# Column sums of the last strip on the tensor engine, and degrees ahead of the split work, in a two-layer graph kernel

## The reference

```python
h  = relu(layernorm(x));  HW = h @ W                   # layer 0
A_norm = relu((adj + adj.T) * 0.5)
D = sum(A_norm, axis=1)
d_inv_sqrt = where(D > 0, D ** -0.5, 0)
L_norm = eye - d_inv_sqrt[:, None] * A_norm * d_inv_sqrt[None, :]
x  = x + relu(L_norm @ HW)
h  = relu(layernorm(x))                                # layer 1, three masks of adj
x  = x + diag(adj) @ (h @ W0) + triu(adj) @ (h @ W1) + tril(adj) @ (h @ W2) + bias
```

## Time and profile before

| | |
|---|---|
| runs | 1016.56, 1022.14, 1025.05 us; median 1022.14 |
| profiled execution | 1022.87 us, span of its records 1021.1 us |
| mean granted TensorE clock | 0.973 of full |
| first pass and passage | up to about 107 us of the span |
| PE busy | 947.7 us, 93% of the span |

### The profile page before, as it was taken

The page is one execution under the profiler, slowest core; times in us unless marked ns, Lnnn a source line. Parts: engine busy times, 40 slices in busy tenths (PEclk is TensorE's granted clock), DMA queues, the critical chain, the costliest instruction groups (busy, mean ns, idle before and its releaser), DMA issues.

```text
span 1021.1 us, 17643 instructions
## 1 busy us (share of the span) xinstructions
PE 947.7 (93%) x4614; PEld 798.9 (78%) x4614; DVE 570.4 (56%) x1491; ACT 499.8 (49%) x1058; POOL 288.0 (28%) x289
## 2 busy tenths in 40 slices
PE   4887889888988999999999999899999999999998
PEld 4776678777777777788888888788888888888886
DVE  5896767567666666656666666544343333433342
ACT  5986446455546555554545555443333333333331
POOL 4785233333333333344344444201111100000000
PEclk9976989999999999999999999999999999999999
DMA  8995678888888887655665555566666665555552
GB/s 238 328 332 142 203 272 267 269 291 278 269 282 277 264 277 237 183 173 169 185 184 171 161 171 166 190 203 203 189 187 183 190 178 165 162 160 167 170 161 74
DMA packets 181210, 213.73 MB, mean 209 GB/s; under 512 B 13616, under 2 KB 116016, under 8 KB 178992
## 3 DMA queue, kind: packets, MB, share of 16 engines
q1 hardware_dynamic: 162736, 171.29, 55.7%
q10 hardware_dynamic: 18432, 41.95, 11.4%
HBM read 145.04 MB, written 68.16 MB: 209 GB/s over the span
## 4 chain that ended last, share of the span: by engine, by line
PE 62%; DMA 12%; issue 7%; ACT 6%; DVE 5%; POOL 5%; SPq 1%; ACTq 1%; DVEq 0%; POOLq 0%
PE psAcc L495 17%; PE psAcc L497 17%; PE psAcc L496 17%; DMA xp<-in_x 6%; DMA s_dram<-C 5%; POOL colacc L920 3%; ACT xp L625 2%; DVE C L714 2%; PE psG L466 2%; PE psG L468 2%; PE psG L467 2%; POOL n_rs L912 1%; PE psZ L428 1%; DVE np_st L697 1%; ACT Yh L619 1%
## 5 line engine op out<-in xcount | busy, mean ns | idle before, releaser
L555 ACT ACTIVATE Lh<-C 128x512 fp32r<-128x512 f32 x256 | 161.4, 631 | 311.3 <-PE psAcc L497 235.4
L495 PE MATMUL psAcc<-Xh,Lh 128*128 128x512 f32 x512 | 208.9, 408 | 6.5 <-DVE Xl L779 4.7
L497 PE MATMUL psAcc<-Xh,Ll 128*128 128x512 f32 x512 | 202.0, 395 | 0.0
L496 PE MATMUL psAcc<-Xl,Lh 128*128 128x512 f32 x512 | 201.6, 394 | 0.0
L495 PE MATMUL psAcc<-Yh,Lh 128*128 128x512 f32 x512 | 200.8, 392 | 0.0
L497 PE MATMUL psAcc<-Yh,Ll 128*128 128x512 f32 x512 | 200.1, 391 | 0.0
L496 PE MATMUL psAcc<-Yl,Lh 128*128 128x512 f32 x512 | 199.9, 390 | 0.0
L723 DVE TENSOR_TENSOR Ll<-C,Lh 128x512 fp32r<-128x512 f32 x128 | 91.0, 712 | 143.8 <-ACT Lh L555 143.7
L495 PEld LDWEIGHTS psAcc<-Xh,Lh 128*128 128x128 f32 x512 | 98.3, 192 | 24.8 <-issue 7.4
L497 PEld LDWEIGHTS psAcc<-Xh,Ll 128*128 128x128 f32 x512 | 97.3, 190 | 21.6
L496 PEld LDWEIGHTS psAcc<-Xl,Lh 128*128 128x128 f32 x512 | 98.3, 192 | 17.7
(11 more groups left out here) (124 smaller groups left out, 1506.5 us busy)
## 6 DMA issues: line engine op xcount, KB each, us to landing
C<-at_dram SPq DMA_DIRECT2D x128, 256.0 KB, 2.7
at_dram<-AT SPq DMA_DIRECT2D x16, 1088.0 KB, 5.5
R<-in_adj SPq DMA_DIRECT2D x64, 256.0 KB, 5.9
C<-in_adj SPq DMA_DIRECT2D x64, 256.0 KB, 3.7
s_dram<-C ACTq DMA_DIRECT2D x64, 256.0 KB, 3.8
g_dram<-g ACTq DMA_DIRECT2D x32, 512.0 KB, 3.5
C<-s_dram SPq DMA_DIRECT2D x64, 256.0 KB, 3.7
xe<-in_x SPq DMA_DIRECT2D x32, 256.0 KB, 3.6
```

The source lines that it names most:

```text
L495: mm(acc, lh, rh[:, k, :], start=k == 0, stop=False)
L496: mm(acc, lh, rl[:, k, :], start=False, stop=False)
L497: mm(acc, ll, rh[:, k, :], start=False, stop=c < L1 and k == NB - 1).then_inc(used, 1)
L555: A(Lh[:, q, :], C[:, q, :], ACT.Relu if s.c < L1 else ACT.Copy).then_inc(lhi, 1)
```

## The change

The changed kernel computes the same degrees with the last strip's column sums made in another way, and places the passage's work in another order.

1. POOL no longer adds strip 15's four chunks to `colacc`. `gathered_sums` takes what strips 1 to 14 have gathered: one matmul with 16 columns of zeros (`d1`), which clears `psD`, and 14 matmuls of one column. It stands on PE between the transposes of chunks (15, 1) and (15, 2). `last_sums(g)` multiplies strip 15's blocks by ones straight from the four slots of `sring`, 15 matmuls of one column in all, and adds them into `psD`. It stands behind `turn0(15)`, ahead of the first `rows_T`.
2. On DVE the four small instructions for the degrees stand ahead of `low0(15)` and of the first `sum_T`; `split_lo(q)` is followed by four of the `Xl` instructions instead of all 16 coming last.
3. On ACT the `Xh` instructions stand in four groups of four between the quarters' splits and copies; on PE `times_W0(14)` comes ahead of the third `rows_T`.

```diff
@@ -178,7 +178,7 @@
             "lxh_ok", "lxl_ok", "g2h_ok", "g2l_ok", "slot_hi", "slot_lo", "acc1", "o_ok")
 
         CH0 = [(k, g) for k in range(NB) for g in range(k // 4 + 1)]
-        BELOW0 = [max(0, min(4, k - 4 * g)) for k, g in CH0]
+        BELOW0 = [max(0, min(4, k - 4 * g)) if k < NB - 1 else 0 for k, g in CH0]
         ADDS0 = [0]
         for w in BELOW0:
             ADDS0.append(ADDS0[-1] + (1 if w else 0))
@@ -354,11 +354,20 @@
             pe.wait_ge(const0, 3)
             pe.wait_ge(d_zero, 2)
 
-            def column_sums():
+            def gathered_sums():
 
                 pe.wait_ge(p0C, ADDS0[-1] + 1)
-                for j in range(NB - 1):
-                    last = mm(psD[:, j:j + 1], colacc[:, j * P:(j + 1) * P], ones[:, :], start=True, stop=True)
+                mm(psD[:, :], colacc[:, 0:P], d1[:, :], start=True, stop=False)
+                for j in range(NB - 2):
+                    mm(psD[:, j:j + 1], colacc[:, j * P:(j + 1) * P], ones[:, :], start=False, stop=False)
+
+            def last_sums(g):
+
+                n = FIRST0[NB - 1] + g
+                pe.wait_ge(p0R, n + 1)
+                for j in range(4 * g, min(4 * g + 4, NB - 1)):
+                    last = mm(psD[:, j:j + 1], sring[:, n % 4, (j - 4 * g) * P:(j - 4 * g + 1) * P], ones[:, :],
+                              start=False, stop=j == NB - 2)
                 last.then_inc(p0D, 1)
 
             def by_W0(dst, hi, lo):
@@ -408,19 +417,21 @@
                     src = rowb[:, k % 3, j * P:(j + 1) * P] if j == k else colb[:, k % 3, j * P:(j + 1) * P]
                     last = nc.tensor.transpose(psA[:, n % 2, (j - 4 * g) * P:(j - 4 * g + 1) * P], src, ident[:, :])
                 last.then_inc(p0T, 1)
+                if (k, g) == (NB - 1, 1):
+                    gathered_sums()
                 if g == k // 4:
                     for m in stages(k):
                         if m >= 4:
                             times_W0(m - 4)
                         if m >= 2:
                             turn0(m - 2)
+            for g in range(NQ):
+                last_sums(g)
             for q in range(2):
-                pe.wait_ge(p0S, len(CH0) - 1 + q)
                 rows_T(Step(None, 0), q)
             times_W0(NB - 2)
-            rows_T(Step(None, 0), 2)
-            column_sums()
-            rows_T(Step(None, 0), 3)
+            for q in range(2, NQ):
+                rows_T(Step(None, 0), q)
             times_W0(NB - 1)
 
             def turn(src, sem):
@@ -568,19 +579,26 @@
                             turned0(m - 2)
                         if m >= 4:
                             got_W0(m - 4)
+            def scaled_hi(i):
+
+                for n in range(4 * i, 4 * i + 4):
+                    act.wait_ge(d_inv, i + 1)
+                    act.wait_ge(hw0, n + 1)
+                    A(Xh[:, n, :], hst[:, n, :], ACT.Copy, scale=scal[:, 0, n:n + 1]).then_inc(prep_hi, 1)
+
             copy_T(Step(None, 0), 0)
             copy_T(Step(None, 0), 1)
+            got_W0(NB - 2)
             split_hi(Step(None, 0), 0)
+            scaled_hi(0)
             copy_T(Step(None, 0), 2)
-            got_W0(NB - 2)
+            split_hi(Step(None, 0), 1)
+            got_W0(NB - 1)
+            scaled_hi(1)
             copy_T(Step(None, 0), 3)
-            got_W0(NB - 1)
-            for q in range(1, NQ):
+            for q in range(2, NQ):
                 split_hi(Step(None, 0), q)
-            for n in range(NB):
-                act.wait_ge(d_inv, n // 4 + 1)
-                act.wait_ge(hw0, n + 1)
-                A(Xh[:, n, :], hst[:, n, :], ACT.Copy, scale=scal[:, 0, n:n + 1]).then_inc(prep_hi, 1)
+                scaled_hi(q)
 
             def gev_out(t, b):
 
@@ -722,7 +740,7 @@
                 else:
                     V.tensor_tensor(Ll[:, q, :], C[:, q, :], Lh[:, q, :].bitcast(F32), ALU.subtract).then_inc(llo, 1)
 
-            V.memset(psD[:, :], 0.0).then_inc(d_zero, 1)
+            V.memset(d1[:, :], 0.0).then_inc(d_zero, 1)
             V.memset(drow[:, :, :], 0.0).then_inc(d_zero, 1)
             V.memset(ones[:, :], 1.0).then_inc(const0, 1)
             dve.wait_ge(whi_ok, 1)
@@ -756,28 +774,31 @@
                             stats(n0s[m % 2], hst[:, m, :], s0_st, s0_mv, s0_ve, m + 1)
                         if m >= 3:
                             low0(m - 3)
-            low0(NB - 1)
-            sum_T(Step(None, 0), 0)
+            def scaled_lo(i):
+
+                for n in range(4 * i, 4 * i + 4):
+                    dve.wait_ge(prep_hi, n + 1)
+                    V.scalar_tensor_tensor(out=Xl[:, n, :], in0=hst[:, n, :], scalar=scal[:, 0, n:n + 1],
+                                           in1=Xh[:, n, :].bitcast(F32), op0=ALU.mult, op1=ALU.subtract).then_inc(prep_lo, 1)
 
             dve.wait_ge(p0R, len(CH0))
             V.reduce_sum(d2[:, :], drow[:, :, :], axis=AX.X).then_inc(d_sums, 1)
             dve.wait_ge(d_sums, 1)
-            dve.wait_ge(p0D, 1)
+            dve.wait_ge(p0D, NQ)
             V.tensor_tensor(d1[:, :], psD[:, :], d2[:, :], ALU.add).then_inc(d_sum, 1)
             dve.wait_ge(d_sum, 1)
-
             V.tensor_scalar(d2[:, :], d1[:, :], 0.0, None, ALU.is_le).then_inc(d_none, 1)
             dve.wait_ge(d_none, 1)
             V.scalar_tensor_tensor(out=dsafe[:, :], in0=d1[:, :], scalar=0.5, in1=d2[:, :],
                                    op0=ALU.mult, op1=ALU.add).then_inc(d_safe, 1)
-            for q in range(1, NQ):
-                sum_T(Step(None, 0), q)
-                split_lo(Step(None, 0), q - 1)
-            split_lo(Step(None, 0), NQ - 1)
-            for n in range(NB):
-                dve.wait_ge(prep_hi, n + 1)
-                V.scalar_tensor_tensor(out=Xl[:, n, :], in0=hst[:, n, :], scalar=scal[:, 0, n:n + 1],
-                                       in1=Xh[:, n, :].bitcast(F32), op0=ALU.mult, op1=ALU.subtract).then_inc(prep_lo, 1)
+            low0(NB - 1)
+            sum_T(Step(None, 0), 0)
+            sum_T(Step(None, 0), 1)
+            for q in range(NQ):
+                split_lo(Step(None, 0), q)
+                scaled_lo(q)
+                if q + 2 < NQ:
+                    sum_T(Step(None, 0), q + 2)
             dve.wait_ge(d_inv, NQ)
             V.scalar_tensor_tensor(out=scal[:, 1, :], in0=scal[:, 0, :], scalar=-0.5, in1=scal[:, 0, :],
                                    op0=ALU.mult, op1=ALU.mult).then_inc(d_ok, 1)
```

## The result

| | before | changed |
|---|---|---|
| median | 1020.77 us (6 runs, 1016.56 to 1025.05) | 1030.75 us (6 runs, 1026.02 to 1034.28) |
| profiled execution | 1022.87 us, span 1021.1 | 1034.28 us, span 1032.6 |
| ratio | | 1.0091, 95% interval 1.0052 to 1.013 |

The time lies in the range, 3 us above the predicted number, and almost on rival C's 1030.7. The profiled execution is the slowest of its six and has the lowest mean granted clock of them (0.961; the others have 0.962 to 0.968), so its 11.5 us are more than the change costs in the median, and the clock that its rows show may be lower than in the others.

A forecast was written before the change was run, and what follows sets the result against it. The prediction took the chain of waits through DVE's last Xl to bound the kernel. Sums read 3.6 us later, 1.2 for two DVE instructions and 0.8 more waiting made 5.6, taken as 5.5: median 1027.6 us, range 1019.5 to 1034.5.

The forecast's parts named there:

- rival C: Clock doesn't return for the second set, which costs 6.3 us instead of 3.3; sum 8.6, median 1030.7 us; chance 0.14.
- What bounds: In the first 110 us the chain of waits decides; a delay of the last Xl moves all later steps by as much.
- The start of the first set: On PE, the first set can't begin before 78.77 us, just behind POOL's adds of strip 14 ending at 78.71.
- The first set, and the dense work behind it: On PE, clock falls a quarter through the set, 5.6 us; the 24 dense instructions then take 5.2 at half clock.
- I let the clock return for the second set: On PE, after 24 dense instructions the second set runs at full clock, 3.3 us; DVE reads the sums at 93.1.
- DVE behind the sums: On DVE, two instructions now behind the sums add 1.2 us and a longer wait for ACT adds 0.8.
- The sum: Whole kernel: 3.6 + 1.2 + 0.8 = 5.6 us slower, taken as 5.5; forecast median 1027.6 us.
- The Trainium skill's rule on transposes: Transposes don't count as a busy PE for the clock; by that rule the clock staying down would be the forecast.
- Rival B: Clock holds at full through both sets; sums read 1.2 us earlier, sum -1.1, median 1021.1 us; chance 0.20.
- Rival D: Clock stays down (8.6 us) and SP's late AT store overlaps the chain's transfers (3.5): 12.1, median 1034.2; chance 0.10.
- The price of a weight load: On PE, the skill's 107 ns whatever the clock would lower the sum some 2.4 us; forecast took 0.21 at half.

The follow-up runs named there:

- x_product_filler: Changed kernel plus 36 unread 128-column split-type matmuls, 8 ahead of the wait for POOL and 14 among each set's sums; ratio 1.0161 to the kernel before.
- x_sums_alone: Changed kernel with its two sets of sums kept but the passage's work in the order of the kernel before; ratio 1.0084 to the kernel before.
- x_late_gather: Changed kernel with the first set of sums moved behind turn0(15), right ahead of the second set; ratio 1.0038 to the kernel before.
- x_two_sets_last: Kernel before with the change's two sets of sums, both behind times_W0(15) on PE, and the degrees behind the splits on DVE; ratio 1.003.
- x_dense_filler: Changed kernel plus 36 unread identity transposes, 8 ahead of the wait for POOL and 14 among each set's sums; ratio 1.005 to the kernel before.

## Why the prediction was right, and the step that failed

- **What bounds.** Right in this pair of profiles: the delay of the last `Xl` (107.4 to 118.94, 11.5 us), of step 1's `sum_T` (11.5) and of the span (11.5) are the same number. That they agree so closely is in part luck. Against the same profile of before, the last `Xl` and the span moved by 16.2 and 18.7 us in x_product_filler and by 10.8 and 9.6 in x_sums_alone, but by 6.2 and 2.4 in x_late_gather and by 3.4 and -2.4 in x_two_sets_last: what comes behind the passage adds or takes up to some 6 us in single executions.
- **The start of the first set.** Forecast 0.06 us behind POOL; it was 1.1 behind (81.18 against 80.08), since PE was late itself: its clock had fallen at 75.4, ahead of the change. In x_sums_alone the set did wait for POOL, 1.09 us, and the clock fell inside it, about 2.8 us after its start at 79.86, where the forecast had it 0.8 after.
- **The first set, and the dense work behind it.** Forecast 5.6 and 5.2 us; measured 6.3 (81.18 to 87.44) and 5.1 (to 92.51). Right in kind; the rest of a microsecond is that the whole set, not three quarters, was at half.
- **"I let the clock return for the second set".** This step failed, in the changed kernel's profile and in that of x_sums_alone. The set took 6.3 us, not 3.3, and the degrees were read at 99.01: 18.9 us behind POOL's strip 14 where the forecast had 14.4 and rival C 17.4. The ground given for it, that the 24 instructions are dense like those of 65.8 to 69.3, mixed two kinds: there 14 of the 17 were transposes, here 12 of the 24 are matmuls of the split type, and x_product_filler shows that such matmuls between the sums don't hold the clock where transposes do. That this is why the clock stayed down behind the first set is likely and not shown: no run has 24 transposes in that place, and in x_product_filler the clock went up behind a stretch that held eight split-type matmuls.
- **DVE behind the sums.** Forecast +2.0 us; measured 118.94 - 99.01 = 19.9 against 17.9, so +2.0. The wait of `split_lo(0)` was 2.28 instead of the 2.9 I had put down, small steps took the rest, so the exact match is luck.
- **The sum.** 5.5 for the forecast and 8.6 for C; measured 9.3 by the ratio. In the profile it is 8.1 up to the degrees, 2.0 behind them, and 1.4 that isn't the change's. The predicted time looks nearer (3 us off) than the predicted change was (4 us off), because the kernel before came out 1.4 us faster than the median it was reckoned from. And 9.3 us could be told from no change, which the forecast had doubted: the interval begins at 5.3.
- **Rival C** had the right time. Its argument from the rows (twelve `h @ W` matmuls at half, and no return) was the good one.
- **The Trainium skill's rule on transposes** ("TensorE: Matmul & The Clock Gate", part 4, PE-mode transpose), that the full clock doesn't engage for them because they don't count as a busy PE in the same way, pointed to C's time for a reason that the runs contradict: with transposes between the sums, x_dense_filler's clock stayed at 1.00 from 76 to 107 us.
- **Rival B** would have needed the clock to hold, and it did not: that is what was wrong with it, and not its other prices. In x_dense_filler's profile, where the clock held, the last column is 0.6 us above before; its 28 fillers in the sets are worth some 1.8 (an estimate, 0.9 a set as above), and without them it would be 1.2 below, close to B's -1.1. Its ratio is 5 us above before, with the runs of low clock in it.
- **Rival D** did not occur: the store of `AT` left SP at 116.82, 9.8 us ahead of the chain's store at 126.61, and took 5.2 us to land, so it was over. Store and load of the chain took 0.8 us more than before all the same; why is open. That two such transfers side by side would take half as long again, D's price, no run here shows.
- **The price of a weight load**, which the Trainium skill ("TensorE: Matmul & The Clock Gate", the section on LDWEIGHTS) gives as columns over 1.2 GHz, 107 ns, with no term for the clock: the second set's 30 one-column records took 6.3 us at half here, 0.21 each, as in the earlier trace rows.

## What to carry to other kernels

Taking work off an engine pays only as far as that engine is what is waited for behind all others: here POOL's four adds could be dropped only by giving PE a second set of matmuls and by holding up the strip behind it, and both lay on the path. In the one profile with the clock held the changed structure was nearly even with before, which suggests that half clock made up most of the loss; the ratios leave room for less. Before an instruction with a long wait is moved earlier, look at which independent instructions of the same engine then stand behind it; the one small gain (3.2 us, interval 0.3 to 6.0) was in the other direction, in filling DVE's wait for the sums with work that had stood behind it. Where a stretch is priced at a granted clock, look up in the trace which kinds of instruction stood ahead of a rise, and not only how busy the engine was. And compare a single profile with the spread of the runs: a difference of a few microseconds between two executions can come from another part of the kernel.

## What the runs showed of the hardware that I had not expected

- TensorE's clock stayed at 1.2 GHz (0.50) while PE was busy without a gap for 30 us (75.4 to 106 in the changed kernel), in a mix of one-column sums, 128-column matmuls of the split type and some transposes. It rose at 106, behind eight transposes and seven split-type matmuls (102.97 to 106.2). With a float32 transpose between the sums it was at 2.4 GHz (1.00) through the same work in x_dense_filler's profile; with a 128-column matmul of the split type in the same place it was not. Whether it is the transpose as such, the float32 type or the values of the operands (the identity against weights) was not separated: the fillers differ in all three. The float32 type is not enough by itself, since the one-column sums at 0.50 are float32 too.
- A one-column float32 matmul is two records of 0.11 us at full clock and 0.21 at half. A 128-column matmul of the split type is one record with the same pitch, so the one-column float32 matmul is twice as dear as the 128-column one of the split type. What is put between the sums has its own price: a transpose in every pair of records came to 0.29 us for the three (81.40 to 85.12 in x_dense_filler), a split-type matmul to 0.34 (82.89 to 85.24 in x_product_filler), both at full clock.
- The moment at which strip 14 is through varies by itself: 78.3 to 82.0 us in twelve profiles of kernels whose work is the same up to there. Runs of the kernel before spread over 16 us (1011.57 to 1027.66); that this and the clock's falls in later steps are the reason is likely and wasn't tried.
